# Values for four pairs in one product, a pair's queries and keys back to back, and another order on every engine, in a two-layer transformer kernel

## What is computed

```python
x = L0_attn_x                                   # (16, 512, 128) float32
xn = _layernorm(x)
x = x + _L0_attn_ref(xn, ...) + _L0_ffn_ref(xn, ...)
xn = _layernorm(x)
x = x + _L1_attn_ref(xn, ...) + _L1_ffn_ref(xn, ...)

# L0 attention: qkv = xn @ w_qkv; sim = q k^T / 8 + slope * -|i-j|, masked; softmax; @ v; @ w_out
# L1 attention: q, k rotated; o = softmax(q1 k1) v - lam * softmax(q2 k2) v; RMS norm per head; @ Wo^T
# FFN: layernorm, (128 x 512) product, silu, (512 x 128) product, residual + 0.5 * z
```

## Time and profile before

| | us |
|---|---|
| median of three runs | 2602.42 (2601.66 to 2603.66) |
| the profiled execution, its own time | 2605.02 |
| span from first to last instruction in it | 2603.2 |
| granted TensorE clock, mean | 0.982 |

### The profile page before, as it was taken

How to read it: one execution, slowest core, us unless ns; L and a number is a source line. 1 busy time by engine, 2 the same in 40 slices (tenths; PEclk the granted TensorE clock), 3 DMA queues, 4 the chain that set the end, 5 groups by cost and what they waited for, 6 DMA issues and landing times.

```text
span 2603.2 us, 52473 instructions
## 1 busy us (share of the span) xinstructions
PE 2442.8 (94%) x18176; PEld 1234.9 (47%) x18176; DVE 1853.8 (71%) x5637; ACT 1886.7 (72%) x4707; POOL 1414.8 (54%) x1353
## 2 busy tenths in 40 slices
PE   6999999999999999999999999999999999999876
PEld 3554444554545445454454544445454444544431
DVE  4448677776877777777776867777687777777664
ACT  4766787777778777777877778777777877777435
POOL 4866474665646565464655647465564646546111
PEclk8999999999999999999999999999999999999977
DMA  3002020100202001020200202011020200102020
GB/s 92 6 5 50 6 54 2 42 18 6 54 6 50 6 18 41 6 54 2 54 6 6 54 6 54 2 36 24 6 54 6 50 6 18 42 2 54 2 53 5
DMA packets 59830, 68.57 MB, mean 26 GB/s; under 512 B 11056, under 2 KB 55344, under 8 KB 56368
## 3 DMA queue, kind: packets, MB, share of 16 engines
q1 hardware_dynamic: 59568, 65.21, 11.0%
HBM read 35.04 MB, written 29.36 MB: 25 GB/s over the span
## 4 chain that ended last, share of the span: by engine, by line
PE 80%; DVE 8%; ACT 7%; issue 3%; POOL 0%; DMA 0%; SPq 0%; POOLq 0%; DVEq 0%; ACTq 0%
PE pj L1348 21%; PE sc L1410 11%; PE pj L1440 11%; PE op L1464 8%; PE sc L1427 6%; PE sc L1497 5%; PE pj L1366 5%; PE sc L1514 5%; PE pj L1454 5%; DVE pq L1112 3%; DVE mx L1165 2%; PE pj L1340 2%; ACT pt L905 2%; ACT pt L883 1%; ACT pq L865 1%
## 5 line engine op out<-in xcount | busy, mean ns | idle before, releaser
L735 POOL TENSOR_SCALAR pq<-pq,rsum 128x128 f32<-128x128 f32 (+3 forms) x1024 | 1115.5, 1103 | 959.6 <-DVE rsum L1119 959.4
L1165 DVE TENSOR_REDUCE mx<-sc 128x1 f32<-128x512 f32 x1024 | 654.6, 682 | 213.4 <-PE sc L1514 212.2
L905 ACT ACTIVATE pt<-sc 128x512 f32<-128x512 f32 x1024 | 557.0, 608 | 198.9 <-PE sc L1497 196.6
L1112 DVE CUSTOM_DVE_ANT_0 pq<-sc,relkey 128x128 f32<-128x128 f32 (+3 forms) x1024 | 450.8, 487 | 222.2 <-PE sc L1410 216.0
L865 ACT ACTIVATE pq<-pq,mx 128x128 f32<-128x128 f32 (+3 forms) x1024 | 571.6, 574 | 6.0 <-DVE mx L1112 6.0
L883 ACT ACTIVATE pt<-sc 128x512 f32<-128x512 f32 (+1 forms) x768 | 356.9, 533 | 229.3 <-PE sc L1427 227.3
L1410 PE MATMUL sc<-K,Q 64*128 64x128 f32 (+3 forms) x2048 | 377.8, 466 | 18.2 <-DVE mx L1165 10.3
L1440 PE MATMUL pj<-pt,v 128*64 128x512 f32 (+3 forms) x2048 | 308.8, 444 | 8.7 <-ACT pt L883 4.2
L1348 PE MATMUL pj<-xnT,wqkv 128*128 128x512 f32 x512 | 282.1, 642 | 11.6 <-ACT xnT L813 5.5
L1464 PE MATMUL op<-pt,v 128*32 128x512 f32 x2048 | 277.1, 613 | 12.7 <-ACT pt L905 12.7
L1514 PE MATMUL sc<-KS,QS 48*128 48x512 bf16 x1024 | 252.0, 389 | 32.9 <-DVE mx L1112 14.2
(11 more groups left out here) (105 smaller groups left out, 2781.3 us busy)
## 6 DMA issues: line engine op xcount, KB each, us to landing
scr_p<-y SPq DMA_DIRECT2D x160, 128.0 KB, 2.4
QS<-scr_p SPq DMA_DIRECT2D x32, 384.0 KB, 6.0
KS<-scr_p SPq DMA_DIRECT2D x32, 384.0 KB, 8.9
x_in<-in_L_attn_x SPq DMA_DIRECT2D x16, 256.0 KB, 2.8
scr_p<-tanh SPq DMA_DIRECT2D x32, 128.0 KB, 2.4
out_x<-xres SPq DMA_DIRECT2D x16, 256.0 KB, 2.3
QS<-nrow SPq DMA_DIRECT2D x192, 4.0 KB
wqkv<-in_L_attn_w_qkv SPq DMA_DIRECT2D x1, 1536.0 KB, 6.7
```

Source lines behind the costliest of these rows:

```text
L735: pool.tensor_scalar(rows, rows, rsum[:, p % NROWS, c:c + 1], None, ALU.mult).then_inc(s_scl, 1)
L905: act.activation(pt1[:, GS * (m % 2) + 2 * j + h, :], sc[tile_bank(i, "st1", 2 * n + h)][:, :], ACT.Exp, scale=float(DS) ** -0.25).then_in ...
L1112: dve.tensor_tensor_reduce(out=pq[:, at:at + width], in0=sc[tile_bank(i, "mx0", m)][:, left:left + width], in1=relkey[:, T - width:T], sca ...
L1165: dve.reduce_max(mx1[:, g % 2, at:at + 1], sc[tile_bank(i, "mx1", 2 * t + h)][:, :], AXIS.X).then_inc(s_mxd1, 1)
```

## The change

- **Values.** `project_v(i, n)` now makes one 512-column product: block k of xnT as weights against the value columns of four pairs. Eight such products a sequence take the place of eight calls with four products each. `v0` holds all eight pairs. They stand in ticks -2, -2, 2, 2, 14, 15, 18, 19 (`V0_AT`) instead of in every tick of kind 2, and ACT copies each with one instruction as before.
- **Queries and keys.** A pair's two projections stand together at the end of tick kind 3, one tick earlier than before, instead of in kind 0 with layer 1's score tiles between them. ACT's `copy_q` moves with them; DVE's `copy_k` stays in kind 0.
- **Norm statistics.** `stats`, `mv`, `veps`, `rstd` have four slots, two for each layer.
- **Order.** Each engine's list in `tick` is rearranged, and some two dozen of the `_AT` constants move by a tick or a few; the numbers of tasks are the same.

```diff
-NBUF = 4
-X_AT = -19
+X_AT = -16
-XNT0_AT = -5
-HT0_AT = -1
-FFN0_AT = (1, 2, 6, 7)
+XNT0_AT = -6
+HT0_AT = 0
+FFN0_AT = (1, 1, 6, 7)
-WOA_AT = 35
-WOB_AT = 45
-LN1_AT = (47, 48, 54)
+WOA_AT = 34
+WOB_AT = 44
+LN1_AT = (48, 49, 54)
-STORE_AT = (49, 50)
-STACK_AT = (54, 54)
+STORE_AT = (50, 50)
+STACK_AT = (56, 60)
-FB_AT = 62
+FB_AT = 63
-TURN_ROPE_AT = (52, 53)
+TURN_ROPE_AT = (52, 54)
-PLN0_AT = (-9, -7)
-PLN1_AT = (47, 48)
-RES0_AT = 0
-RES1_AT = 53
+PLN0_AT = (-10, -7)
+PLN1_AT = (48, 49)
+RES0_AT = 5
+RES1_AT = 52
-STOREOUT_AT = 89
+STOREOUT_AT = 95
+V0_AT = (-2, -2, 2, 2, 14, 15, 18, 19)
...
-        stats = sb("stats", [P, 2, NT, 6])
+        stats = sb("stats", [P, 4, NT, 6])
...
-        v0 = sb("v0", [P, NBUF, NT, P])
+        v0 = sb("v0", [P, NPAIR, NT, P])
...
-            def project_v(i, p):
-                project(i, f"v{p}", lambda k: xnT[:, P * k:P * (k + 1)], lambda k: wqkv[:, 2 * INNER + P * p:2 * INNER + P * (p + 1)], NT)
+            def project_v(i, n):
+                half, k = divmod(n, NT)
+                if n == 0:
+                    b, u = pj_use(i, "xnT0")
+                    pe.wait_ge(s_pje[b], u)
+                at = 2 * INNER + HP * P * half
+                project(i, f"v{n}", lambda _: xnT[:, P * k:P * (k + 1)], lambda _: wqkv[:, at:at + HP * P], 1)
...
```

More of the change, by code:

```diff
@@ L289, in pj_order @@
             second(h, 0)
+            second(h, 1)
             pairs("pv", g, 3)
             misc(g, h)
-            second(h, 1)
         elif r == 2:
             second(h, 0)
-            pairs("v", g, -1)
             misc(g, h)
@@ L299, in pj_order @@
             second(h, 0)
+            misc(g, h)
             second(h, 1)
-            misc(g, h)
+            pairs("q", g, -2)
+            pairs("k", g, -2)
     return order
@@ L786, in tick @@
                         scale_probs(i, p, 0)
+                    small(g, h)
+                elif r == 2:
                     small(g, h)
@@ L925, in others @@
                     transposed(i, 0, "h")
+                for n in range(2 * NT):
+                    if (i := at(g, V0_AT[n])) is not None:
+                        values(i, n)
                 for f in range(NF):
@@ L960, in tick @@
                         exp0(i, p, 3)
-                    p, i = pair(g, -1)
-                    if i is not None:
-                        copy_q(i, p)
                     p, i = pair(g, 2)
@@ L992, in tick @@
                         exp0(i, p, 1)
+                elif r == 2:
+                    second_attention(h, 0)
                     second_attention(h, 1)
-                    p, i = pair(g, -1)
-                    if i is not None:
-                        values(i, p)
                     others(g, h)
@@ L1010, in tick @@
                     second_attention(h, 1)
+                    p, i = pair(g, -2)
+                    if i is not None:
+                        copy_q(i, p)
             pipeline(tick)
@@ L1305, in tick @@
                         row_max0(i, p, 2)
-                    norms(g)
-                    others(g, h)
+                    p, i = pair(g, 0)
+                    if i is not None:
+                        invert_sums(i, p, 0)
+                    second_attention(h, 0)
+                    second_attention(h, 1)
+                    norms(g)
+                else:
+                    p, i = pair(g, 0)
+                    if i is not None:
+                        row_max0(i, p, 3)
+                    norms(g)
                     second_attention(h, 0)
@@ L1533, in others @@
                     transpose4(i, "hT0", lambda k: hn[:, k, :])
+                for n in range(2 * NT):
+                    if (i := at(g, V0_AT[n])) is not None:
+                        project_v(i, n)
                 for f in range(NF):
@@ L1595, in tick @@
                         turn_probs(i, p, 1)
+                    others(g, h)
                     second_values(h, 0)
-                    second_values(h, 1)
-                    others(g, h)
                     p, i = pair(g, 2)
@@ L1609, in tick @@
                         pv0(i, p)
+                    second_values(h, 0)
+                    second_keys(h, 1)
+                    others(g, h)
+                    second_values(h, 1)
+                    second_tops(h, 1)
+                    p, i = pair(g, 0)
+                    if i is not None:
+                        max_scores0(i, p, 2)
+                elif r == 2:
                     second_keys(h, 0)
+                    second_turns(h, 0)
                     second_tops(h, 0)
-                    second_values(h, 0)
                     others(g, h)
@@ L1646, in tick @@
                         turn_probs(i, p, 0)
+                    second_turns(h, 1)
+                    second_tops(h, 1)
                     second_values(h, 1)
                     second_keys(h, 1)
-                    second_tops(h, 1)
+                    p, i = pair(g, -2)
+                    if i is not None:
+                        project_q(i, p)
+                        project_k(i, p)
             pipeline(tick)
```

134 lines of the change are left out of this document (52 added, 82 removed).

## The result

The changed kernel takes 2619.73 us (median of 4 runs, 2616.61 to 2620.84) against 2602.04 (2598.23 to 2603.66) for the one before, run beside it: a ratio of 1.006, with an interval of 1.0046 to 1.0074. It is slower by 0.6%, where the forecast was 2541. The profiled execution took 2616.61, its span is 2614.8.

A forecast was written before the change was run, and what follows sets the result against it. PE's time per sequence, waits included, was taken as the bound. Work -4.9 and waits +0.6 gave -4.3 a period; over the whole run -69.6 + 14 x 0.6 = -61, so 2541 us, range 2520 to 2560 (0.52).

The forecast's parts named there:

- Waits: 10.3 - 1.5 + 2.1 = 10.9: PE's waits per period: 10.3 us before, 1.5 expected to go and 2.1 to come, leaving 10.9.
- Queries and keys together, -1.4: On PE, seven more pairs joined, each taking 1.92 instead of 1.06 + 1.05, saves 1.4 us a period.
- the fifth rival: On PE only groups in different rows overlap, so adjacent full-array products save nothing; -2.3 a period, 2570; chance 0.02.
- Values, -0.27 and -0.6: On PE, eight 512-column products at 1.06 instead of 1.09 (-0.27); three more full-array products meeting another (-0.6), per period.
- Score products moved, -1.5 and -1.1: Without q, k, v between PE's score groups: 15 more same-row neighbours (-1.5), 11 cheaper `max_scores0` groups (-1.1) a period.
- Waits that go, -1.5: On PE per period: hT0 fills waits between `turn_probs` 1 and 2 (-0.5); top groups and FFN products get separated (about -1).
- (a): LN1's statistics and POOL's part a tick later, xnT1 unmoved on PE: a wait of +0.5 us, from 0 to 2.
- (b): KS stack's DMA before the first top group: PE has 1.2 us less work ahead, slack 2.5 covers most; +0.3.
- (c): k's bank, freed by DVE in kind 0, at pair 6 only after `rotate`, delays the second rotary product; +0.5.
- (d): Window 884.29 to 905.07: ACT, busy 18.23 of 20.78, becomes as long as PE there; +0.8.
- The third: Kind 3 writes ten score tiles in a burst over five banks; twelve ticks wait, +0.6 each: period 157, 2635; chance 0.07.
- Rival 2: DVE and ACT, reading score banks, take most back: waits grow by 3, only 1.9 a period stays, 2575; chance 0.17.

The follow-up runs named there:

- a_rope: Changed kernel with DVE's rotation of the keys a tick earlier and POOL's second residual a tick later, both as in the kernel before; 2618.9 us, one execution.
- a_woa: Changed kernel with the first `attention_out` a tick later, as in the kernel before; 2613.71 us, one execution.
- c_join: Kernel before with q and k together between `turns0` and `max_scores0(0)`, kind 3's single tasks at the tick's end, `second_values(h, 1)` ahead of them; 2801.18 us, 1.0759.

## Why the prediction was wrong, point by point

**The step that failed** is the sum of waits: "Waits: 10.3 - 1.5 + 2.1 = 10.9". Measured, 17.2: 16.6 of waits, and 0.6 of a clock at its lower level, for which the prediction had no term. The prediction took q, k and v for work that "cut through" the score tiles and priced their leaving by what PE's own groups then cost, 2.6 us of the 4.9. It never asked what those projections had been covering. With them between, the five banks came free in time: in the rows on which the argument stood, k at 886.12 and `max_scores0(0)` behind it begin with no idle time. And the kernel before has the same run without cover once in a period, in tick 9, where the top pair waits 0.72 for the exponential (the 7.8 us in 14 times above). The prediction counted this among its 10.3 and did not ask why there was only one of it. In the changed kernel there are six, and the five new ones hold 3.8 us.

*Queries and keys together, -1.4.* The size is right: 1.91 to 1.96 in all eight pairs, but for the four periods in which the clock falls on the pair of tick 3. That also settles the fifth rival. The Trainium skill, "TensorE: Matmul & The Clock Gate", section "Part 3: Packing small matmuls", lets a weight load run beside matmuls in flight only when the rows differ. By that rule q and k together would have gained nothing and taken 2.11. The trace disagrees. But what the part is worth in the changed kernel is seen with it undone: 14.2 of waits instead of 17.2, a ratio of 1.0027 instead of 1.006.

*Values, -0.27 and -0.6.* The work fell by 1.2 with the values alone, a little more than these two sum to. By place, the wide product is worth nothing measurable (0.9992), and its move costs 5.3 more of waits (16.1 against 10.8), an estimated 1.1 of it the clock.

*Score products moved, -1.5 and -1.1.* The first holds within 20 ns a group. The second was mis-sized: `max_scores0(0)` behind a top pair costs 0.73 undisturbed and 0.76 behind k, 0.03 less where I took the 0.10 of `max_scores0(2)`. Seven of them make 0.2, not 0.7, and that is the difference between the 4.9 and the 4.4 measured.

*Waits that go, -1.5.* The top groups in a row did stop waiting: ticks 11, 29 and 30 lose 1.9. The 0.5 for hT0 between two `turn_probs` did not come: they wait 0.77 in tick 0 with hT0 between (0.63 before), and 0.84 in tick 8 (0.61 before).

*Waits that come.* (a) xnT1, +0.5: it waits 0.3 a period, but not for the reason given. POOL's power ends at 1264.70; DVE comes to xn only at 1267.95, behind other work of its own, and ends at 1269.26, and xnT1 begins at 1269.32:

```profile
PE pj L1340 <- DVE xn L1073: 3.3, 13, 0.3
```

Near it the key pair ahead of `pv0` waits 0.35 too. (b) The KS stack: no wait before the first top group. (c) The bank of k and the rotation, +0.5: the right mechanism, too small. In tick 20 `pv0` of pair 2 waits 1.4 for a projection bank that DVE's rotation frees; the tick has 1.8 where it had 0.5. (d) ACT, +0.8 "in that window": the right engine, at the wrong scale. I read how busy ACT was over 20.78 us; what counts is that one exponential stands 1.2 us from the key pair's start to the free bank, and PE has 0.45 to put there.

**The rivals.** The third ("score tiles in a burst", 0.07, 2635) is what happened: waits past its 15.2, a period of 157.2 where it said 157, on the slow side. That the period fits so well is in part luck: the growth is not spread over its twelve ticks, and 0.6 of it is the clock. Two things in it were not as written. The burst that matters is kind 0's and kind 2's, key, top and score products over five banks, not kind 3's ten tiles; and "q and k now follow the burst and give DVE 1.9 us" counted against it, while for the run behind q and k they come too early to be cover. Rival 2 had the right direction (ACT and DVE take it back) and stopped at 3 us, for which nothing in the rows spoke. The time of rival 3, 2635, missed by 15, since the start of the run gained 14.5, which the per-period sum (x 14) does not hold.

**What is shown and what is argued.** Shown: the work fell by 4.4; the recurring wait of 0.72 to 0.78 is for the first key tile's bank, and follows the exponential one for one (0.213 for 0.220). Of the +6.8, the five new places of this shape hold 3.8. Tick 16's wait is the exponential's too (0.38 to 0.06 when it is shorter), and so is part of tick 17's (0.35 to 0.14). Shown by one place each: tick 20 (`a_rope`, 1.0) and 0.4 of tick 3 (`a_woa`). 0.6 is the clock, read from its rows. Ticks 28 and 0 (+1.1) have the same run of groups, but over top tiles, whose reader is DVE; they did not move with the exponential and are put down to the ring by likeness alone. Open: why the clock falls in four periods and not in the others, and which of its edits makes `c_join` so dear. The periods of the changed kernel vary between 156.1 and 158.9, while before's hold 154.76 nearly always: the four long ones are the four in which the clock falls.

## What to carry to other kernels

Before work is taken from between tiles that share a ring of banks, write out for each run of n + 1 tiles over n banks the time from the first tile's start to its bank being free, reader included, and compare it with what the engine itself has to fill it (here 1.23 against 0.45). If it is more, whatever stands between is cover, and to take it away gains nothing up to that difference; shares of busy time over a period or even over 20 us (ACT 73%) don't show it. Look at the granted clock of every period, not of one: here it fell behind such waits in four periods of thirteen, and a window on one of the others showed 1.00. When banks are handed out in turn, moving one task also changes which tasks share a bank: two kernels here lost 1.66 us a period to a neighbour that was moved in on q1.

## What the runs showed that I had not expected

The time that small operations of DVE take goes with what POOL runs beside them. The three 128x128 products of the layer's last norm take 0.26, 0.29 and 0.29 in the kernel before (at 954.32) while POOL scales; in the changed kernel, in one tick, they stand beside two of POOL's tensor-tensor operations. First DVE's, then POOL's timeline of that stretch:

```profile
1441.55 0.80 DVE L1189 TENSOR_TENSOR sq<-dif,rms 128x128 f32<-128x128 f32 x1
1442.38 1.31 DVE L1193 TENSOR_TENSOR ow<-sq,lnw 128x128 f32<-128x128 f32 x1
1443.72 0.66 DVE L1196 TENSOR_TENSOR o<-ow,lnw 128x128 f32<-128x128 f32 x1
```

```profile
1440.93 1.27 POOL L719 TENSOR_TENSOR xacc<-xacc,xn 128x512 f32<-128x512 f32 x1
1442.27 1.27 POOL L723 TENSOR_TENSOR xacc<-xacc,bias 128x512 f32<-128x512 f32 x1
```

Over all 64, the middle one's mean goes from 359 to 586 ns, with a median of 293 or 294 in both. Beside POOL's scaling it is not always short either: up to 0.69. It is about 1.9 us of DVE in that tick (2.77 less 0.84), right before the rotation on which `pv0` of pair 2 waits. In `a_rope`, where POOL's residual stands a tick later, the middle one never takes more than 0.48, and the wait in tick 20 is 1.0 shorter. That run moved the rotation a tick as well, so how much of the 1.0 is the slow products' is not shown.
